# A graph network layer on one core: from pair 20 on, the table gathers of a pair wait for the adds of the pairs in front

## What is computed

```python
ts = edge_weight[:, None]
ef = relu(edge_attr_64 @ We1 + be1) @ We2 + be2      # 64 -> 128 -> 128 channels
ef = ef * sigmoid(ts @ Wt + bt)
combined = concatenate([x[src], ef], axis=1)         # 256 channels
msg = relu(combined @ Wn1 + bn1) @ Wn2 + bn2
out = segment_sum(msg, dst, num_segments=6250)
result = layernorm(x + (out + x))
```

## Time and profile before

| what | value |
|---|---|
| median of 3 runs | 1063.53 us (1062.24 to 1064.23) |
| the profiled execution, its own time | 1062.49 us |
| its span, first to last instruction | 1060.7 us |
| POOL busy | 789.8 us, 841 instructions |
| PE busy | 852.4 us |
| DVE busy | 649.3 us |
| ACT busy | 589.0 us |
| mean granted TensorE clock | 0.953 |

### The profile page before, as it was taken

How to read it: one execution, slowest core, us unless ns; L and a number is a source line. 1 busy time by engine, 2 the same in 40 slices (tenths; PEclk the granted TensorE clock), 3 DMA queues, 4 the chain that set the end, 5 groups by cost and what they waited for, 6 DMA issues and landing times.

```text
span 1060.7 us, 15682 instructions
## 1 busy us (share of the span) xinstructions
PE 852.4 (80%) x5031; PEld 618.9 (58%) x5032; DVE 649.3 (61%) x1688; ACT 589.0 (56%) x649; POOL 789.8 (74%) x841
## 2 busy tenths in 40 slices
PE   6899998688787787797778787878777877877884
PEld 6667666466565466465556555656454655654664
DVE  4767775655755745655556466566466565657566
ACT  5576766546555546455546555556455554655542
POOL 7777777777777777777777777777777777777773
PEclk9999999989999999889999999999999998999897
DMA  8965555444544444444444444444444444445211
GB/s 246 291 206 162 157 164 141 125 142 122 150 136 138 129 139 131 129 149 122 133 143 133 131 142 132 133 143 133 132 135 131 140 129 137 142 122 146 79 52 52
DMA packets 78756, 148.46 MB, mean 140 GB/s; under 512 B 19175, under 2 KB 47014, under 8 KB 78662
## 3 DMA queue, kind: packets, MB, share of 16 engines
q1 hardware_dynamic: 49446, 89.26, 25.9%
q0 software_dynamic: 26624, 54.58, 20.2%
q10 hardware_dynamic: 2592, 3.48, 0.9%
HBM read 140.85 MB, written 6.40 MB: 139 GB/s over the span
## 4 chain that ended last, share of the span: by engine, by line
POOL 62%; issue 21%; PE 6%; DVE 4%; DMA 4%; ACT 2%; SPq 1%; DVEq 0%; ACTq 0%; POOLq 0%
POOL gathered L485 62%; DMA gathered<-node_table,src_e 2%; PE psS L755 2%; PE psM L796 2%; DMA x_sb<-in_x 1%; DVE h L1075 1%; PE psH L809 1%; ACT h L543 1%; DVE onehot L1081 0%; ACT tw L598 0%; PE psE L821 0%; SPq L400 0%; DVE gathered L949 0%; DVE span_f L939 0%; PE psS L887 0%
## 5 line engine op out<-in xcount | busy, mean ns | idle before, releaser
L485 POOL DMA_INDIRECT gathered<-node_table,src_e x800 | 758.3, 948 | 244.9 <-issue 241.0
L606 ACT ACTIVATE h<-psH,be_c 128x1024 f32<-128x1024 f32 x104 | 115.9, 1114 | 340.0 <-PE psH L809 339.9
L755 PE MATMUL psS<-onehot,h 128*128 128x128 f32 x1656 | 226.7, 293 | 94.6 <-ACT h L543 91.9
L1075 DVE TENSOR_TENSOR h<-psM,gathered 128x1024 f32<-128x1024 f32 (+1 forms) x104 | 122.8, 1182 | 276.3 <-DMA gathered<-node_table,src_e 251.4
L755 PEld LDWEIGHTS psS<-onehot,h 128*128 128x128 f32 x1656 | 209.5, 204 | 112.7 <-ACT h L543 57.8
L598 ACT ACTIVATE tw<-ew,bt_c,wt_c 128x1024 f32<-128x1024 f32 x104 | 235.8, 2268 | 11.8 <-DVE efw L1096 11.6
L821 PE MATMUL psE<-h,we 128*128 128x512 f32 x416 | 215.8, 643 | 0.0
L796 PE MATMUL psM<-wn,efw 128*128 128x128 f32 x1664 | 212.0, 283 | 4.8 <-DVE h L1075 4.8
L796 PEld LDWEIGHTS psM<-wn,efw 128*128 128x128 f32 x1664 | 204.1, 200 | 5.6 <-DVE h L1075 5.6
L1096 DVE SCALAR_TENSOR_TENSOR efw<-psE,be_c,tw 128x1024 f32<-128x1024 f32 x104 | 133.1, 1280 | 77.6 <-PE psE L821 76.5
L1081 DVE TENSOR_SCALAR onehot<-split_ids,dst_e 128x65 f32<-128x65 f32 x832 | 173.8, 271 | 0.0
(11 more groups left out here) (111 smaller groups left out, 336.8 us busy)
## 6 DMA issues: line engine op xcount, KB each, us to landing
ew<-in_edge_weight SPq DMA_DIRECT2D x104, 512.0 KB, 3.8
ea<-in_edge_attr SPq DMA_DIRECT2D x104, 256.0 KB
gathered<-node_table,src_e POOLq DMA_INDIRECT x800, 2.9
x_sb<-in_x SPq DMA_DIRECT2D x6, 512.0 KB, 9.4
out_y<-x_sb ACTq DMA_DIRECT2D x12, 256.0 KB
node_table<-gathered SPq DMA_DIRECT2D x7, 256.0 KB
node_table<-h SPq DMA_DIRECT2D x4, 256.0 KB, 3.9
h<-in_x,raw_e POOLq DMA_INDIRECT x16, 5.9
```

The lines of the kernel that those rows point to most:

```text
L485: pool.indirect_dma_start(to, None, rows, bass.IndirectOffsetOnAxis(index, 0)).then_inc(landed, 16)
L606: nc.scalar.activation(h1[:, s % 2, :], psH[:, :, :].rearrange("p r e -> p (r e)"), ACT.Relu, bias=be1_c[:, :]).then_inc(h1_ready, 1)
L755: return nc.tensor.matmul(to, h[:, (k - SUM_LAG) % BODY * PAIR + q, t * C:(t + 1) * C], hot, start=(t == 0), stop=(t == TILES - 1))
L1075: return nc.vector.tensor_tensor(to, of, rows, ALU.add)
```

## The change

From pair 20 (`CLOSE_FROM`) to the last, the first gather of pair p waits until pair p - 2 is added (`pre_ready >= p - 1`) in place of pair p - 4. In addition the fifth gather waits until pair p - 1, directly in front, is added (`pre_ready >= p`), so that the fifth to eighth gather are behind that. Each wait is carried by a no-operation on POOL. Pairs 4 to 19 are as before; no instruction of another engine changes.

```diff
+CLOSE_FROM = 20
...
             for p in range(RAW // PAIR, PAIRS):
-                if p >= RAW // PAIR + BODY:
+                if p >= CLOSE_FROM:
+                    pool.wait_ge(pre_ready, p - 1)
+                    pool.nop(nofuse=True)
+                elif p >= RAW // PAIR + BODY:
                     pool.wait_ge(pre_ready, p - (BODY - 1))
                     pool.nop(nofuse=True)
                 for q in range(PAIR):
+                    if q == 1 and p >= CLOSE_FROM:
+                        pool.wait_ge(pre_ready, p)
+                        pool.nop(nofuse=True)
                     for t in range(TILES):
```

## The result

The changed kernel takes 1069.49 us (median of 8 runs, 1066.76 to 1071.87), the kernel before 1063.32 us (8 runs, 1062.24 to 1064.23): 6.2 us slower between the medians, 0.6%; the ratio of the runs is 1.0055 with a 95% interval of 1.0045 to 1.0066. The prediction was 1069. The runs of the changed kernel also spread wider, 5.1 us against 2.0.

The account below looks back on a forecast made before the run. POOL's unbroken gathers, 1.25 us each, were taken to bound the kernel. Five holds sum to 5.6 us; added to the median 1063.5 they give 1069.1, stated as 1069 us, range 1064.8 to 1076.

Parts of the forecast that it names:

- POOL sets the pace, and a delay of it is never made up: POOL hands out gathers without a break, 1.25 us each, 10.0 a pair; no other slack in front of the last gather.
- A met wait is free, the first gather's never binds: POOL's waits: one already met costs 0, hidden in the 0.30 us gap; the first gather's new value never holds POOL.
- The price, 0.74 us from the add's end to the gather: Unmet wait on POOL: next gather starts 0.74 us after the add's end, read at pair 8; lower bound 0.30.
- the add is over before POOL even reaches the no-operation, and I count nothing: Fifth gathers starting 0.30 to 0.75 us after the add's end, as at pair 95: counted as no hold.
- The sum, 5.6 us: Holds before fifth gathers of pairs 24, 44, 50, 65, 89: 1.97, 1.81, 0.70, 0.49, 0.65 us; bounds 3.4 and 10.3.
- the 1.7 and 3 us that it left out: Upper-bound extras: 1.7 us if six pairs at 0.30 to 0.75 us paid; 3 if late neighbours were not spared.
- The late adds beside the first holds: Late adds around the first two holds (pairs 21, 24 and 44) cost nothing more, POOL being already moved 1.97 or 1.81 us.
- The time in hand, 2.2 us: Ordinary pair: add ends 3.6 to 4.1 us after the last gather starts; next fifth gather due at 6.25, some 2.2 spare.
- A hold breeds no further ones: Load-and-add loop takes 9.1 us against POOL's 10.0, so lateness shrinks 0.9 us a pair; nothing is late after a hold.
- No difference: Rival: late adds come from few accidents; two big holds fall out, 0.5 us left, 1064 us; chance 0.16.
- Every pair exposed: Rival: POOL-DVE loop with longest landing 4.5 takes 10.2 us, each of 84 pairs loses 0.2: 17 us, 1080; chance 0.07.
- Faster: Rival: closer coupling thins transfers in flight, gathers shorten, POOL wins 2.0 us with nearly no holds: 1061.5; chance 0.05.

## Why the prediction was right, point by point

**POOL sets the pace, and a delay of it is never made up.** Right. In every profile the gathers keep 0.95 + 0.30 us, and the held time reappears in the time: 6.1 us of holds against 6.2 between the medians, 38.2 against 37.8, 96.8 against 96.9, 2.8 against 2.7.

**A met wait is free, the first gather's never binds.** Right, by the second wait for an old add (0.9997) and the first gather's wait alone (0.9999).

**The price, 0.74 us from the add's end to the gather.** Right, it is 0.75 at all ten holds. But the step "the add is over before POOL even reaches the no-operation, and I count nothing" failed. The 0.75 us are due wherever the distance is under 0.75, also while POOL is still busy with the gather in front: holds of 0.15, 0.21, 0.28 and 0.39 us came of it, 1.0 us of the 6.1. Of the two readings that the prediction set side by side, the one it left to the upper bound holds.

**The sum, 5.6 us.** It measured 6.1 in the profile and 6.2 by the medians. That it came so near is partly luck: the executions differ. Late adds fall on other pairs from one to the next; two profiles with the fifth gather's wait have 6.1 and 10.2 us of holds, and the times spread over 5 us. Counted in full (0.75 us due everywhere, nothing spared beside a hold), the execution that the prediction read gives 10.3 us in 15 pairs, its own upper bound; the three other traces without a hold give 10.6, 6.0 and 4.6. It read an execution with many late adds, and the 1.7 and 3 us that it left out brought the sum back to the median. The list of five places was a sample of a distribution, not the places to come: of pairs 24, 44, 50, 65 and 89 only 89 was held. What the profile would show was off in the same way: ten gaps of 0.45 to 1.36 us, where five to eight, two of them near 2.2, were named, and 11.2 us put down to DVE in place of 7 to 9. Adds that start over 4 us behind the eighth gather did not become rarer: five before, five after.

**The late adds beside the first holds.** This step is wrong in its order. Pair 22, whose wait is for the add of 21, comes before pair 24, so POOL had not been moved yet when it reached it; in the kernel before its fifth gather starts just as that add ends (229.86). It was held in the changed run, 0.82 us. By the prediction's own rule the sum stays, as a hold at 22 would be taken off the one at 24.

**The time in hand, 2.2 us.** Too large. In the kernel before the distance from an add's end to the next pair's fifth gather is 1.8 us in the middle, since a pair's last gather lands after 3.1 us in the middle. The 2.4 and 2.9 of the earlier trace rows are the shortest and the median of the 58 gathers whose landing that view knows. The list of held pairs was read from the rows and did not use it.

**A hold breeds no further ones.** Nothing speaks against it. Four of the ten holds stand in neighbouring pairs (21 and 22, 72 and 73), which the prediction had named as a sign of being wrong; but adds late by over 3 us stand side by side in the kernel before too (20 to 24, 43 and 44, 94 and 95, among others). At the fifth and at the fourth gather the held time is no more than the distances of the traces without a hold give. At the third it is less, and the adds are less late, in the direction of the room that the prediction spoke of. Its working, 0.9 us less lateness a pair, was not tested: it holds against a POOL that does not yield, and the estimated loop through POOL with the wait before the fourth gather, 9.6 us (0.75 + four periods + 2.6 + 1.22), leaves 0.4. That late neighbours cost nothing extra, as the sum assumed, is not borne out.

**The rivals.** "No difference" needs adds that are not late; that was made by taking away the load (1.0009) or by moving the wait one gather on (1.0005). "Every pair exposed" is real, but two gathers away: there the loop took the 10.8 us of its formula. "Faster" did not happen; the gathers took 0.9 us less, and nothing shows that the waits did that.

**Early issue.** The Trainium skill (DMA: Bandwidth & Descriptors, Rules for kernel authors) says to issue a DMA early and wait late. The runs agree in direction, with a measure: the closeness costs nothing with the wait before the sixth gather, 6 us before the fifth, 38 before the fourth and 97 before the third.

## What to carry to other kernels

A wait put on the engine that sets the pace costs nothing as long as its condition is met some 0.75 us before the instruction behind it would start; compare the whole distribution of distances with that, and over several executions, not the mean of one. Here a distance of 1.8 us in the middle left ten of 84 pairs to pay for, and other executions of the same kernel work out at 5 to 11 us. Each such loss is final on the pacing engine. Where a loop through a transfer is closed, work out its length at the longest landing that the trace shows, and look which other transfer is issued beside it: cutting that one removed nearly all of the loss without touching the wait.

## What the runs showed of the hardware that was not expected

A semaphore that arrives while POOL is still busy with a gather is not free: the add ended 0.29 us before the fourth gather's end, and the gap behind grew from 0.30 to 0.45 us. A guess, shown by no run: some 0.7 us of the next gather's handling normally overlap the gather in front and cannot begin until the wait is met. The profile shows the length only, in a single "issue" piece of 0.70 us.

With a load of 512 KB per pair on another queue, the last 64 KB gather of a pair lands after 3.1 us in the middle; with 64 KB per pair, after 2.5. That shift of the middle goes with 22 late adds in place of 5.
